# Gated cross-attention block: the first attention units start inside the last projection job, output tiles alternate between two PSUM banks

## The reference, cut to what matters

```python
x = x + tanh(g_xattn) * xattn(layernorm(x), ctx, mask)   # x, ctx: 8 batches x 128 tokens x 512
x = x + tanh(g_ffn)  * ffn(layernorm(x))

def xattn(h, kv, mask):                    # 32 heads of 128
    q = rmsnorm(h) * ln_weight @ w_q.T;  k = kv @ w_k.T;  v = kv @ w_v.T
    p = softmax(q @ k.T + position_bias, where mask)      # per head, 128 x 128
    return h + (p @ v) @ w_out.T

def ffn(y):                                # base linear layer, plus rank-16 LoRA of 8 experts
    w = top-8 router probabilities, mapped to experts     # 15 router outputs
    return y @ base_W.T + base_b + sum_e w[e] * (y @ A[e].T) @ B[e].T * 2
```

## Time and profile before

| | |
|---|---|
| Time, median of 3 runs | 892.32 us (890.05 to 893.9) |
| The profiled execution | 891.21 us |
| Its span, first to last instruction | 889.4 us |
| Busy: PE / DVE / ACT / POOL | 845.3 / 670.7 / 499.1 / 487.3 us |
| Mean granted PE clock, as a share of full speed | 0.984 |
| Busy share of the 16 DMA engines, by the page's third part | 75.6% (q1) |

### The profile page before, as it was taken

The page is one execution under the profiler, slowest core; times in us unless marked ns, Lnnn a source line. Parts: engine busy times, 40 slices in busy tenths (PEclk is TensorE's granted clock), DMA queues, the critical chain, the costliest instruction groups (busy, mean ns, idle before and its releaser), DMA issues.

```text
span 889.4 us, 13885 instructions
## 1 busy us (share of the span) xinstructions
PE 845.3 (95%) x4204; PEld 706.6 (79%) x4204; DVE 670.7 (75%) x1174; ACT 499.1 (56%) x1185; POOL 487.3 (55%) x352
## 2 busy tenths in 40 slices
PE   6999999989999996999999999999999999977998
PEld 5877888768888884888888888888888888856786
DVE  6887777866766645888888888888888888859864
ACT  6556676666676643555555555655655555525310
POOL 0355334644466523666666666766666666646432
PEclk9999999999999998999999999999999999998999
DMA  8867677569877787889889898888888988974101
GB/s 289 307 238 284 258 263 280 205 261 356 301 272 279 274 314 236 249 242 259 235 239 259 239 256 248 249 261 244 241 255 250 253 252 248 272 214 133 46 25 71
DMA packets 155393, 214.73 MB, mean 241 GB/s; under 512 B 10960, under 2 KB 109392, under 8 KB 154960
## 3 DMA queue, kind: packets, MB, share of 16 engines
q1 hardware_dynamic: 155344, 214.13, 75.6%
HBM read 128.11 MB, written 85.98 MB: 241 GB/s over the span
## 4 chain that ended last, share of the span: by engine, by line
DVE 37%; PE 37%; ACT 12%; issue 7%; DMA 5%; DVEq 1%; SPq 1%; POOL 0%; ACTq 0%; POOLq 0%
ACT p_exp L738 10%; DVE p_norm L1067 6%; PE Sb L1331 5%; PE Sb L1333 5%; PE Sb L1332 5%; DVE s_sb L1050 4%; DVE negmax L1052 4%; DVE rscale L1062 4%; DVE V_lo L898 4%; DVE s_sb L1048 4%; DVE acc L1082 3%; PE Ab L1331 2%; PE Ab L1332 2%; PE Ab L1333 2%; DVE unit_out L898 2%
## 5 line engine op out<-in xcount | busy, mean ns | idle before, releaser
L467 POOL TENSOR_TENSOR w_lo<-w_raw,w_hi 128x1280 fp32r<-128x1280 f32 (+1 forms) x29 | 85.2, 2938 | 122.5 <-ACT w_hi L604 122.5
L511 POOL TENSOR_TENSOR a_rest<-small_a,A_hi 128x512 f32<-128x512 f32 x64 | 82.9, 1296 | 124.3 <-ACT small_a L732 124.2
L738 ACT ACTIVATE p_exp<-s_sb,negmax 128x128 f32<-128x128 f32 x256 | 99.8, 391 | 56.3 <-DVE negmax L1052 56.1
L1322 PE MATMUL Ob<-o_hi,A_lo 128*128 128x512 f32 x248 | 101.0, 407 | 17.5 <-DVE acc L1095 11.4
L516 POOL TENSOR_TENSOR P_hl<-pT,P_hl 128x512 fp32r<-128x512 f32 x64 | 83.0, 1297 | 39.5 <-ACT P_hl L604 39.0
L1323 PE MATMUL Ob<-o_lo,A_hi 128*128 128x512 f32 x248 | 98.2, 396 | 0.0
L1324 PE MATMUL Ob<-o_hi,A_hi 128*128 128x512 f32 x248 | 98.1, 396 | 0.0
L504 POOL TENSOR_TENSOR bm<-bias,maskneg 128x512 f32<-128x512 f32 x64 | 83.8, 1309 | 24.6 <-DVE s_sb L1048 24.6
L604 ACT ACTIVATE P_hl<-pT 128x512 fp32r<-128x512 f32 x64 | 40.5, 633 | 76.0 <-DMA pT<-p_rows 75.9
L604 ACT ACTIVATE U<-Sb 128x512 f32<-128x512 f32 x90 | 53.6, 599 | 47.1 <-PE Sb L1333 46.4
L604 ACT ACTIVATE A_hi<-Ab 128x512 fp32r<-128x512 f32 x64 | 38.4, 599 | 72.4 <-PE Ab L1492 72.4
(11 more groups left out here) (292 smaller groups left out, 2605.2 us busy)
## 6 DMA issues: line engine op xcount, KB each, us to landing
qk_units<-unit_out SPq DMA_DIRECT2D x128, 512.0 KB, 3.0
qk<-qk_units SPq DMA_DIRECT2D x64, 1024.0 KB, 7.2
p_rows<-p_blocks SPq DMA_DIRECT2D x64, 256.0 KB, 2.6
pT<-p_rows SPq DMA_DIRECT2D x256, 64.0 KB, 4.4
w_raw<-wqk SPq DMA_DIRECT2D x31, 512.0 KB, 4.3
v_raw<-wv SPq DMA_DIRECT2D x32, 256.0 KB, 4.8
o_raw<-wo SPq DMA_DIRECT2D x32, 256.0 KB, 5.0
stage<-ctxT SPq DMA_DIRECT2D x8, 256.0 KB, 6.2
```

Of the source, the lines that this page charges most:

```text
L467: pool.tensor_tensor(w_lo[:, n % 2, first:5, :], w_raw[:, n % 2, first:5, :], f32(w_hi[:, n % 2, first:5, :]), ALU.subtract).then_inc(w1_l ...
L738: last = act.activation(p_exp[:, i, :], s_sb[:, i, :], ACT.Exp, bias=negmax[:, i:i + 1], accum_out=rowsum[:, i:i + 1])
L1322: pe.matmul(dst, w_lo, m_hi, start=start, stop=False)
```

## The change

Five edits. Unit numbers are counted from 0.

- **Early scores.** The scores of units 0 and 1 are computed inside and right behind the last job 31, into the bank QP, as three matmuls of 128 columns per head instead of one of 256 and one of 128. The softmax of unit 0 (DVE, ACT) stands in job 31, that of unit 1 between the last results of the first phase. The order of the following steps up to unit 3 is written out by hand on all engines. PE's `m3(30)` and ACT's `c12_hi(30)` move forward to make room, and SP has a list of its own (`first_units`).
- **Two banks for output tiles.** Even batches use Ob, odd ones QP. The output product of unit u now waits for `acc_done` of u-1 instead of u. The banks of the last group are reordered.
- **Base weights sooner.** Their load moves from b = 4 to b = 3 of the last group, their splits from b = 4 to 7 to b = 5 to 7 and behind the exponentials, the fourth behind the loop.
- **K to Q order.** At n = 16, DVE and ACT make the block c21 of job 15 (`unit_lo(R21, 15)`) ahead of c22's low half and c11, and DVE's split of T4 stands behind c11.
- **Statistics of x.** Those of the second half are spread over jobs 4 to 9, one tile each.

Besides, `pt_done`, `ld_wv` and `ld_o` become several semaphores, one per buffer or tile, and some tiles in SBUF change places.

```diff
+EARLY = 2
 ...
+        def o_bank(b):
+            return (Ob[:, :], QP[:, :])[b % 2]
-        out_bank = [Ob[:, :]] * 4 + [Vb[:, :], Ob[:, :], Vb[:, :], Ob[:, :]]
+        out_bank = [Ob[:, :], QP[:, :], Ob[:, :], Vb[:, :], Ob[:, :], Vb[:, :], Ob[:, :], Vb[:, :]]
 ...                                                        # SP
+            def first_units():
+                for i in range(4):
+                    sp.wait_ge(st[i], 16 * (G + 2))
+                sp.wait_ge(scores_done, 1)
+                load_unit(0, 2)
+                store_blocks(0, 0)
+                load_blocks(0, 0)
+                sp.wait_ge(scores_done, 2)
+                load_unit(0, 3)
+                store(R22, JOBS - 1)
+                store(R21, JOBS - 1)
+                store_blocks(0, 1)
+                sp.wait_ge(m_done[4], J(JOBS - 1))
+                load_wv(1, 1, 0)
+                load_blocks(0, 1)
+                sp.wait_ge(scores_done, 3)
+                load_unit(0, 4)
+                store(R12, JOBS - 1)
+                load_wv(1, 1, 1)
+                load_bias(1, 1)
+                store_blocks(0, 2)
+                load_blocks(0, 2)
+                load_wv(1, 1, 2)
+                sp.wait_ge(scores_done, 4)
+                load_unit(0, 5)
+                load_wv(1, 1, 3)
-                    if last and b == 4:
+                    if last and b == 3:
                         sp.wait_ge(o_done, LAST)
                         sp.dma_start(base_raw[:, :, :], baseT).then_inc(ld_base, 16)
 ...                                                        # ACT, step
-                if last and b >= 4:
+                exponentials(t)
+                if last and b >= 5:
                     act.wait_ge(ld_base, 16)
-                    late_high(w_base_hi[:, b - 4, :], base_raw[:, b - 4, :])
-                exponentials(t)
+                    late_high(w_base_hi[:, b - 5, :], base_raw[:, b - 5, :])
 ...                                                        # ACT, behind job 31
+            exponentials(2)
+            probs_hi(0, 0, 1)
+            v_evict_hi(1, 1)
+            v_evict_hi(2, 2)
+            attention_hi(0, 0)
+            small_attention(0)
+            probs_hi(1, 1, 1)
+            v_evict_hi(3, 3)
+            split_wv_hi(1, 1, 0)
+            exponentials(3)
+            split_wv_hi(1, 1, 1)
+            split_wv_hi(1, 1, 2)
-            for b in range(B):
+            for b in range(4, B):
                 step(0, b, 0)
 ...                                                        # DVE
+            def scores_early(u):
+                reached(dve, exp_done, u)
+                dve.wait_ge(scores_done, u + 1)
+                dve.wait_ge(bm_done, u + 1)
+                dve.tensor_tensor(s_sb[:, :, :], heads(QP[:, :]), bm[:, :, :], ALU.add).then_inc(first_sum_done, 1)
+                dve.wait_ge(first_sum_done, u + 1)
+                dve.tensor_reduce(negmax[:, :], s_sb[:, :, :], AX.X, ALU.max, negate=True).then_inc(max_done, 1)
+                if n == JOBS - 1:
+                    scores_early(0)
+                    normalise(0, 0)
+                    transpose_blocks(0)
                 if n == G:
-                    x_sum_lo(T4)
+                    unit_lo(R21, n - 1, X[(n - 1) % 2])
                 if n > PLAIN:
                     unit_lo(R22, n - 1, C22)
                 c11(n)
+                if n == G:
+                    x_sum_lo(T4)
 ...                                                        # PE
-                    if late and b == 4:
+                    if isinstance(u, int) and u == 1:
+                        pe.wait_ge(first_sum_done, EARLY)
+                    if late and b == 3:
                         pe.wait_ge(v_lo_done, UNITS - 1)
-                    elif late and b > 4:
+                    elif late and b > 1:
                         pe.wait_ge(f_x1, b - 1)
-                    elif late and b > 0:
-                        pe.wait_ge(f_x1, b)
                     else:
-                        reached(pe, acc_done, u)
+                        reached(pe, acc_done, u - 1)
+            def scores_early(u):
+                pe.wait_ge(ld_qk[u % 2], 16)
+                reached(pe, first_sum_done, u)
+                for h in range(HU):
+                    K_hl, Q_hl = qk[:, u % 2, h, 0, :], qk[:, u % 2, h, 1, :]
+                    pe.matmul(QP[:, tok(h)], Q_hl[:, S:2 * S], K_hl[:, 0:S], start=True, stop=False)
+                    pe.matmul(QP[:, tok(h)], Q_hl[:, 0:S], K_hl[:, S:2 * S], start=False, stop=False)
+                    last = pe.matmul(QP[:, tok(h)], Q_hl[:, 0:S], K_hl[:, 0:S], start=False, stop=True)
+                last.then_inc(scores_done, 1)
+                if n == JOBS - 1:
+                    m3(n - 1)
+                    scores_early(0)
                 m6(n)
-                if n > PLAIN:
+                if n > PLAIN and n < JOBS - 1:
                     m3(n - 1)
 ...
+            scores_early(1)
             v_half(0, 0, 0, 0, 0)
             m4(JOBS - 1)
             v_half(0, 0, 0, 0, 1)
-            v_half(1, 0, 1, 0, 0)
-            scores(0, 0, 0)
             m3(JOBS - 1)
-            v_half(1, 0, 1, 0, 1)
-            for b in range(1, B):
+            scores(2, 0, 2)
+            for b in (1, 2):
+                v_half(b, 0, b, 0, 0)
+                v_half(b, 0, b, 0, 1)
+            apply_probs(0, 0)
+            v_half(3, 0, 3, 0, 0)
+            v_half(3, 0, 3, 0, 1)
+            for b in range(3, B):
                 step(0, b, 0)
```

More of the change, by code:

```diff
@@ L161, in build @@
         ld_bias = sem("ld_bias")
-        ld_bb, ld_wv, ld_o = sem("ld_bb"), sem("ld_wv"), sem("ld_o")
+        ld_bb = sem("ld_bb")
+        ld_wv, ld_o = ([ld_c[k][c] for k in range(4)] for c in range(2))
         ld_qk = [sem("ld_qk0"), sem("ld_qk1")]
@@ L395, in _ @@
                     store(R12, n - 1)
+            def first_units():
[24 more added lines that the diff above has]
+                load_wv(1, 1, 3)
             def group(g, q):
                 first, last = (isinstance(g, int) and g == n for n in (0, GROUPS - 1))
-                for b in range(B):
-                    if first and b == 0:
-                        for i in range(4):
-                            sp.wait_ge(st[i], 16 * (G + 2))
+                for b in range(4 if first else 0, B):
                     if first and b == 4:
@@ L406, in group @@
                     before = (g, b - 1) if b > 0 else (g - 1, B - 1)
-                    if not (first and b == 0):
-                        store_blocks(*before)
+                    store_blocks(*before)
                     if not (last and b >= B - 2):
@@ L411, in group @@
                         load_unit(g + (b + 2) // B, (b + 2) % B)
-                    if not (first and b == 0):
-                        load_blocks(*before)
-                    if first and b == 0:
-                        sp.wait_ge(m_done[4], J(JOBS - 1))
+                    load_blocks(*before)
                     if b < DC and not last:
@@ L572, in _ @@
             bias_and_mask(0, 0, 0)
-            for b in range(B):
+            bias_and_mask(0, 1, 0)
+            bias_and_mask(0, 2, 0)
+            bias_and_mask(0, 3, 0)
+            probs_lo(0, 0)
+            a_remainder(0, 0)
+            probs_lo(1, 1)
+            split_wv_lo(1, 1, 0)
+            bias_and_mask(0, 4, 0)
+            split_wv_lo(1, 1, 1)
+            split_wv_lo(1, 1, 2)
+            for b in range(4, B):
                 step(0, b, 0)
@@ L816, in _ @@
                     c21_hi(n - 1)
+                    exponentials(1)
                     v_evict_hi(0, 0)
@@ L831, in _ @@
                 c11_hi(n)
[L832 removed]
+                if n > PLAIN and n != G:
                     c21_hi(n - 1)
+                if n == JOBS - 1:
+                    c12_hi(n - 1)
                 if n != G:
@@ L1175, in _ @@
                 if n == JOBS:
+                    scores_early(1)
                     unit_lo(R22, n - 1, C22)
                     unit_lo(R21, n - 1, X[(n - 1) % 2])
+                    c12(n - 1)
+                    normalise(1, 1)
+                    transpose_blocks(1)
                     v_evict_lo(0, 0)
-                    c12(n - 1)
+                    scores(2)
                     unit_lo(R12, n - 1, C12)
@@ L1194, in _ @@
                 if n == 3:
+                    for i in range(BH):
+                        tile_stats(0, i)
                     layernorm_stats(0)
@@ L1223, in _ @@
                     router_constants()
-            for b in range(B):
+            v_evict_lo(1, 1)
+            normalise(2, 2)
+            transpose_blocks(2)
+            v_evict_lo(2, 2)
+            attention_lo(0, 0)
+            v_evict_lo(3, 3)
+            scores(3)
+            normalise(3, 3)
+            transpose_blocks(3)
+            for b in range(4, B):
                 step(0, b, 0)
@@ L1452, in out_half @@
```

(16 more changed lines are left out.)

89 lines of the change are left out of this document (52 added, 37 removed).

## The result

| | before | after |
|---|---|---|
| Median of 20 runs | 893.4 us | 883.4 us |
| Ratio of the times | | 0.9907 (0.9882 to 0.9932) |
| The profiled execution | 891.21 us | 882.73 us |
| Its span | 889.4 us | 880.9 us |
| Mean granted clock | 0.984 | 0.986 |

The change makes the kernel 0.9% faster, 8 to 10 us. The forecast was 20.1 us, 872 us, with a range up to 881: less than half of the gain came, and the measured time lies 2.4 us beyond the range.

What follows compares the result with a forecast made beforehand. PE, busy 845 of 889.4 us, was taken as the bound, with DVE's list and ACT setting the units' pace. Terms 1.7 + 0.9 + 8.0 + 0 + 9.5 = 20.1 us gave 872 us, range 864 to 881.

Steps and rivals of the forecast that it cites:

- the third bullet of the switch: First units: the third wv tile lands near 356; ACT loses 2 to 3 us, PE about 2; from none to 5.
- paid after: PE's remaining costs where the first phase passes to the units: 2.7, 0.9 and 2.0 us, set against 13.5 before.
- the switch gives its lead back: First units: ACT's list is held up, only statistics and base weights remain, 11 to 12 us; 880 us, chance 0.14.
- third term: Passage to the units: 8.0 us gained (5 to 10.3); false if the loop's first unit moves by less than 5 us.
- Early softmax: End of the first phase: unit 0's softmax and transposition done near 329.8 instead of 342.2, 12.4 us sooner.
- The term for the early scores: Scores of units 0 and 1: 24 matmuls instead of 16 cost PE 0.9 us; by the skill's figure 0.1 or 0.2.
- K to Q: Around job 16: the 4.1-us wait ends 3.7 us sooner, a new one precedes m4(16); gain 0.9 us (0 to 3.5).
- Statistics: Early jobs of the second half: PE's two 0.7-us waits go with their restarts; gain 1.7 us (0 to 1.9).
- Loop: Middle units, two banks: PE's small waits go but DVE sets the pace; gain 0, from -3 to +7.
- the 7 of the rival: Loop: exponentials wait for scores that wait for PE, so 5.4 to 7 us come off as well; 865 us, chance 0.10.
- Base weights: Last group: ACT's wait for the base weights goes whole, taking 9.5 us off DVE's chain; from 7.8 to 11.
- the slower rival: Loop: earlier ACT and POOL work collides with p_norm, 1.05 us per unit; up to 928 us, chance 0.04.

Runs made afterwards that it cites:

- one bank's waits: The changed kernel, still with two banks, but its output products wait as in the kernel before; ratio to the kernel before 0.9901 (0.9874 to 0.9928).

## Why the prediction was wrong

**The step that failed** is the third bullet of the switch: "`load_wv(1, 1, 2)` [...] Issued at about 351, with 4.8 us to land, it is there near 356; [...] ACT loses 2 to 3 us there, PE about 2." It was issued at 358.69 and split at 363.50, and ACT lost 7.25 us there and 5.2 for pT(1), for which the sum had nothing. I had priced every transfer by its own median from the table of issues: 2.5 us for the blocks' store, 4.8 for a tile. Those medians are of the loop, where 1.75 MB go in a step of 7.5 us and the blocks' store is issued ahead of the 1-MB load. The change starts the units while job 31's results are still to be stored, and puts 2 MB ahead of each of two small stores on which the whole chain hangs. The rows for it stood in the prediction (1 MB of a unit takes 7.2 us); what I did not do is to add up what is ahead of a transfer in the queue. Even my bound for this bullet, 5 us, named only one 1-MB load.

In the account that the sum used, "paid after" was 5.6 us. PE's waits from 340 to 380 us add up to 12.5, and the granted clock is 0.50 from 364.5 to 374.6, in and behind the longest of them, where PE is busy for 5.9 us. The account had the low clock in what was paid before and no term for it in what is paid after.

**The rival "the switch gives its lead back"** is what happened, by the mechanism named there (pT(1) and the late tiles hold ACT), with 0.14 where it deserved the most. It was sized as a loss of the 8 us, which gave 880; it took 11.5 from the forecast. The sign that the prediction had set for a false third term, a loop that starts less than 5 us sooner, is there.

**Early softmax**: 12.4 us forecast to the end of unit 0, 12.3 measured. The exponentials of unit 2 ended and P_hl(0) started at 339.1, directly behind, as said (342.5 forecast; 2.6 of the difference are the lead up to matmul 1320). The term for the early scores holds too: on PE their matmuls of 128 columns begin 0.11 us apart, as those of 144 columns do, so 8 more of them cost the 0.9 us and not the 0.1 or 0.2 of the prediction's second estimate:

```profile
325.46 0.28 PE L1588 MATMUL QP<-qk 128*128 128x128 f32 x1
325.57 0.27 PE L1589 MATMUL QP<-qk 128*128 128x128 f32 x1
```

**K to Q**: the 4.1-us wait became 0.4, and a wait of 2.15 us stands before m4(16), inside the forecast 1.9 to 3.0; 1.1 us saved, 0.9 forecast, with the low clock assumed. What ends the wait is ACT's snapshot, not T4's low half, which was done at 179.70:

```profile
177.99 1.71 DVE L960 TENSOR_TENSOR t_lo<-stage,t_hi 128x1024 fp32r<-128x1024 f32 x1
...
180.22 0.68 DVE L1021 TENSOR_TENSOR Ob<-Kb,U 128x512 f32<-128x512 f32 x1
```

The split took 1.71 us, between the 1.22 and the 2.4 of the forecast, and DVE had no idle time between it and c12 (`Ob<-Kb,U`), on which the snapshot waits. So the slow split did cost some 0.5 us, by another way than the forecast's.

**Statistics**: 1.7 forecast, 0.2 measured. The 0.7-us waits went, but new ones of 0.4 and 0.2 us for xn came in the jobs behind, and one of 0.33 us for ACT's U at 36 us, which two other runs with this edit have as well. In the seven runs with this edit and without that wait 0.6 to 0.8 us are saved. The granted clock is 1.00 from 12 to 172 us in both kernels, so it has no part in this.

**Loop**: 0 forecast. 2.6 measured in one pair of profiles, some 2 over all runs, well inside -3 to +7 and not the 7 of the rival; 2.3 of the 2.6 are shorter durations of DVE's own instructions. DVE does set the pace: from 380 to 780 us it waits for the exponentials 53 times, 59.4 us in all, where it was 59.1, and again never for PE.

**Base weights**: 9.5 forecast and measured when alone, 7.1 in the changed kernel. DVE's reciprocal waits 1.4 us in all there. Of the 2.4 us less, 1.9 went into DVE's own durations in the last group, above all unit 61's p_norm and unit 62's rscale, here after:

```profile
798.67 1.74 DVE L1138 TENSOR_TENSOR p_norm<-p_exp,rscale 128x512 f32<-128x512 f32 x1
...
808.74 1.14 DVE L1133 TENSOR_TENSOR rscale<-rinv,valid 128x4 f32<-128x4 f32 x1
```

and in the run with the base weights alone:

```profile
801.04 0.69 DVE L1069 TENSOR_TENSOR p_norm<-p_exp,rscale 128x512 f32<-128x512 f32 x1
...
809.65 0.16 DVE L1064 TENSOR_TENSOR rscale<-rinv,valid 128x4 f32<-128x4 f32 x1
```

That is the slower rival's mechanism, in one group and not in the loop: there p_norm is long in 3 of the 51 units from 8 to 58, and was in 7 before. On POOL, meanwhile, first in the changed kernel and then with the base weights alone:

```profile
797.07 1.56 POOL L534 TENSOR_TENSOR bm<-bias,maskneg 128x512 f32<-128x512 f32 x1
798.58 1.29 POOL L551 TENSOR_TENSOR o_lo<-o_raw,o_hi 128x512 fp32r<-128x512 f32 x1
```

```profile
801.11 1.78 POOL L504 TENSOR_TENSOR bm<-bias,maskneg 128x512 f32<-128x512 f32 x1
```

In the changed kernel p_norm starts 0.09 us behind the low half of the first base tile (`o_lo<-o_raw,o_hi`), an instruction that the edit put there, and takes 1.74. With the base weights alone it starts 0.07 us ahead of POOL's `bm`, and it is `bm` that is long: 1.78 us, where the median of its 64 is 1.29. The Trainium skill ("SBUF — State Buffer", section "Who interferes with whom") has it that such a DVE instruction with two SBUF inputs and a reading GpSimd instruction exclude each other. The 1.74 and the 1.78 agree. What of the 2.4 us is this edit's own and what the banks' order stays open: with one bank's waits the 1.74 was still there.

## What to carry to other kernels

Starting a chain earlier was worth nothing here, because its small transfers queued behind the bulk of the phase that it now overlaps: before moving a step, write down the bytes that stand ahead of each of its DMAs, and issue the small ones that others wait for first. Work that is needed late, as a split of the next weights, must not stand in an in-order list ahead of the chain, however early its data should be there. And an edit that removes a plain wait at the critical place (one load issued a step sooner) can be worth all the others together.

## What the runs showed that I had not expected

The clock behind a short idle time is not settled by the code around it. Ten of the kernels have the same code around job 16 and wait 2.14 to 2.17 us before m4(16). In five of them, the changed kernel among them, the granted clock was then low (1.2 GHz for part of 6 us); in the other five it stayed at 2.4 GHz, here in the run with one bank's waits (all engines: PE, its weight loads, DVE, ACT and POOL):

```profile
182.00:185.00 3.00, 3.00 (x14) 2.45 (x15) 2.84 (x7) 1.92 (x3) 0.00 (x0) 1.00 1.03 373
185.00:188.00 3.00, 3.00 (x15) 2.49 (x14) 2.33 (x4) 2.30 (x5) 2.71 (x1) 1.00 1.00 332
```

Matmuls 660 to 780 take 30.9 us in these and 32.5 in the others. What decides it no run here shows. Something like it happens behind unit 63, where the stretch to the end took 61.4 to 61.8 us in six profiles and 63.3 to 66.4 in six others; the waits differ a little there, but the time weighted by what the clock lacked is 0 to 1.8 us in the six short ones and 1.7 to 5.4 in the long ones. Single profiles differ by up to 5 us through this, as much as half of what this change brings. That is why the stages were compared piece by piece and not by spans.
